# First stage of a graph kernel: message products in quarters of the PE array, with a new order of PE's work

## The reference

```
h = silu(edge_attr_16 @ Wfc1/4);   w = h @ Wfc2/8          # 192 weights: w0, w1 (64 each), w2, w3 (32 each)
e0 = (x0 @ Wl1_0 * a / 8)[src];    e1 = (x1 @ Wl1_1 * a / sqrt(32))[src]
mid0 = w0 * e0 * sh0;              mid1 = w3 * (e1 . sh1) / sqrt(3)
mid2 = w1 * e0 * sh1;              mid3 = w2 * e1 * sh0
```

## Time and profile before

| | us |
|---|---|
| median of 3 runs | 903.74 (903.16 to 905.57) |
| profiled execution: time | 900.12 |
| its span | 898.4 |
| PE busy | 845.2 (94%) |
| DVE busy | 810.1 (90%) |
| POOL busy | 713.5 (79%) |
| ACT busy | 628.3 (70%) |

### The profile page before, as it was taken

How to read it: one execution, slowest core, us unless ns; L and a number is a source line. 1 busy time by engine, 2 the same in 40 slices (tenths; PEclk the granted TensorE clock), 3 DMA queues, 4 the chain that set the end, 5 groups by cost and what they waited for, 6 DMA issues and landing times.

```text
span 898.4 us, 33828 instructions
## 1 busy us (share of the span) xinstructions
PE 845.2 (94%) x11276; PEld 713.2 (79%) x11276; DVE 810.1 (90%) x2797; ACT 628.3 (70%) x1961; POOL 713.5 (79%) x804
## 2 busy tenths in 40 slices
PE   2999899999999999999999988999999999999994
PEld 1788788888887887888888877888888888888884
DVE  3798899999998999999999987999999999999997
ACT  1555455555555555565565554999999999999998
POOL 6777777777777776777777711999999999999995
PEclk9999999999999999999999999999999999999998
DMA  6455544544557676557764412899999999999994
GB/s 184 122 169 168 153 134 137 139 129 130 133 145 151 187 209 182 174 163 204 210 179 133 130 69 101 249 307 311 317 299 309 332 332 305 311 319 307 316 310 159
DMA packets 87544, 186.85 MB, mean 208 GB/s; under 512 B 17646, under 2 KB 48138, under 8 KB 87371
## 3 DMA queue, kind: packets, MB, share of 16 engines
q1 hardware_dynamic: 50715, 93.00, 31.9%
q0 software_dynamic: 18944, 35.81, 18.1%
q10 hardware_dynamic: 17712, 55.87, 18.1%
HBM read 119.66 MB, written 64.95 MB: 205 GB/s over the span
## 4 chain that ended last, share of the span: by engine, by line
PE 50%; DVE 14%; SPq 12%; issue 12%; DMA 6%; POOL 4%; ACT 2%; DVEq 0%; ACTq 0%; POOLq 0%
PE ps L831 9%; SPq L467 9%; PE ps L772 7%; PE ps L751 6%; PE ps L732 5%; PE ps L769 5%; PE ps L738 5%; DVE mid L1024 4%; PE ps L817 3%; SPq L457 3%; DVE z L1042 3%; PE ps L714 3%; PE ps L847 3%; PE ps L712 3%; POOL gat L620 2%
## 5 line engine op out<-in xcount | busy, mean ns | idle before, releaser
L620 POOL DMA_INDIRECT gat<-turned,srcs x196 | 192.2, 981 | 65.6 <-issue 61.2
L620 POOL DMA_INDIRECT gat<-spread,srcs x196 | 187.7, 958 | 62.4 <-issue 59.1
L901 ACT ACTIVATE te<-ps 128x512 f32<-128x512 f32 x196 | 106.4, 595 | 123.7 <-PE ps L738 120.8
L831 PE MATMUL ps<-win,eas 60*128 60x162 f32 x2352 | 190.0, 306 | 1.1 <-DVE eas L1367 0.7
L772 PE MATMUL ps<-wy,mid 128*128 128x161 f32 x784 | 182.3, 314 | 0.0
L831 PEld LDWEIGHTS ps<-win,eas 60*128 60x128 f32 x2352 | 165.6, 186 | 18.0 <-DVE eas L1367 11.0
L1048 DVE SCALAR_TENSOR_TENSOR msg<-ps,sha,z 128x161 f32<-128x161 f32 x392 | 151.0, 385 | 13.9
L686 POOL TENSOR_TENSOR gat<-eas,gat 128x640 f32<-128x640 f32 x98 | 152.0, 1551 | 10.9 <-ACT eas L946 10.5
L769 PE MATMUL ps<-wy,mid 128*128 128x97 f32 x784 | 141.6, 262 | 0.2 <-DVE mid L1024 0.2
L1024 DVE TENSOR_TENSOR mid<-ps,te 128x512 f32<-128x512 f32 x196 | 133.3, 680 | 3.3 <-PE ps L751 3.3
L924 ACT ACTIVATE te<-gat,shift,rstd 128x160 f32<-128x160 f32 x292 | 131.8, 533 | 2.7 <-DVE shift L1314 1.3
(11 more groups left out here) (110 smaller groups left out, 1501.1 us busy)
## 6 DMA issues: line engine op xcount, KB each, us to landing
win<-rows SPq DMA_DIRECT2D x392, 114.6 KB, 4.0
rows<-msg SPq DMA_DIRECT2D x98, 326.0 KB
out<-te ACTq DMA_DIRECT2D x47, 640.0 KB, 6.6
xin<-x_g ACTq DMA_DIRECT2D x76, 322.0 KB, 5.7
kept_x<-x_g SPq DMA_DIRECT2D x16, 322.0 KB
gat<-turned,srcs POOLq DMA_INDIRECT x196
gat<-spread,srcs POOLq DMA_INDIRECT x196
eas<-ea_t SPq DMA_DIRECT2D x7, 384.0 KB, 3.8
```

What stands on the lines that cost most here:

```text
L620: pool.indirect_dma_start(out=gat[:, slot, first:first + of.shape[1]], out_offset=None, in_=of, in_offset=bass.IndirectOffsetOnAxis(ap=src ...
L831: last = nc.tensor.matmul(agg_ps[b1][:, 2 * h + k, 0:SW], hot[side(h), b1, k, c, :], win[side(h), (RING * i + b - 1) % WIN_RING, k, c, 0:S ...
L901: nc.scalar.activation(e_sb[:, t, :], e_ps[:, t], ACT.Copy).then_inc(e_out[t], 1)
```

## The change

**PE, y products.** `combine` cuts each product of a tile into quarters: rows of the weights' input in two halves, and edges in two halves. Products with zero blocks of the weights are left out. A pair takes 16 products of 64 rows by 64 edges with 32, 66 or 99 columns. The outputs lie in banks 6 and 7, in 16 lanes of 33 numbers (`CHUNK`), the two tiles' lanes in turn; a product writes one, two or three lanes. Products from the lower half of the rows write bank 6, those from the upper half bank 7.

**Banks and waits.** Both pairs use banks 6 and 7, so `combine` waits for the messages of the pair just before it (`msg_ready[t], p`). The banks of e hold nothing else, and e waits for no message.

**Order on PE.** y of pair 0, first layer, transposes of both pairs, y of pair 1, e, w. On ACT `take_second` stands ahead of `take_turned`; on DVE both `multiply` follow `finish` of pair 0.

**ACT and DVE.** `take_second` copies 132 numbers for both tiles at once. `finish` makes two products for a pair, 128 and 64 numbers (32 for each tile and component), and then one message product for each tile. A message is 165 numbers wide, five chunks of 32 and one (count, label, gate, one unused), where it was 163; the label is written into `z` and goes through the message product. The node stage multiplies 164 columns in L831, and ACT takes the 160 sums out of five chunks. Tables, weights and the output's columns are put in another order outside the kernel's loops.

```
-GATE, CNT, LABEL = 0, 1 + D, 2 + D
-SW = 2 + D
-AW = 3 + D
+CHUNK = MUL1 + 1
+CHUNKS = 5
+AW = CHUNKS * CHUNK
+SW = AW - 1
+
+
+M_A, M_C, M_S, M_B = 0, CHUNK, 2 * CHUNK, 4 * CHUNK
+CNT, LABEL, GATE = M_A + MUL1, M_C + MUL1, M_S + MUL1
...
-        y_ps = [ps[:, n:n + 2, 0:YW] for n in (2, 6)]
-        heads_ps = ps[:, 6:8, YW:YW + T // 2]
-        wrong_ps = ps[0:1, 6, YW + T // 2:YW + T // 2 + 1]
+        heads_ps = ps[:, 6:8, 0:T // 2]
+        wrong_ps = ps[0:1, 6, T // 2:T // 2 + 1]
+
+        y_ps = ps[:, 6:8, :].rearrange("p c e -> p (c e)")
+
+        def y_at(t, j, count=1, every=1):
+
+            flat = y_ps
+            lanes = flat[:, 512 - YB:512 + YB].rearrange("p (j t w) -> p j t w", t=2, w=CHUNK)
+            return lanes[:, j + 4:j + 4 + (count - 1) * every + 1:every, t, :]
...
+            def find_e(q):
+                b = q % 2
+
+                pe.wait_ge(t_out, 2 * q + 2)
+                if q >= 1:
+                    for t in range(2):
+                        pe.wait_ge(e_out[t], q)
+                for n in range(2):
+                    for t in range(2):
...
             def combine(q, k):
-                p, y = 2 * q + k, y_ps[k]
-                if p == 1:
+                p = 2 * q + k
+                if p == 0:
                     pe.wait_ge(heads_out, 2)
+                    pe.wait_ge(wy_ready, 12)
                 for t in range(2):
-                    if p == 0:
-                        pe.wait_ge(wy_ready, 12)
                     pe.wait_ge(mid_ready[t], q + 1)
-                    if k == 0:
-                        pe.wait_ge(e_out[t], min(q + 2, NS))
-                    if q >= 1:
-                        pe.wait_ge(msg_ready[t], p - 1)
-                    nc.tensor.matmul(y[:, t, 0:W_Y1 - W_YA], mid[:, q % 2, t, 0, k, :],
-                                     wy[:, 0:W_Y1 - W_YA], start=True, stop=True)
-                    of = (W_Y1, W_Y1B)[t] - W_YA
-                    nc.tensor.matmul(y[:, t, W_Y1 - W_YA:YW], mid[:, q % 2, t, 1, k, :],
-                                     wy[:, of:of + VEC + 1 + MUL0],
-                                     start=True, stop=True).then_inc(y_ready[t], 1)
+                    if p >= 1:
+                        pe.wait_ge(msg_ready[t], p)
+
+
+                low, high = slice(0, HALF), slice(HALF, P)
+                made = ((0, 0, low, W_V, y_at(0, -4)[:, :, 0:MUL1]),
+                        (0, 0, high, W_YA, y_at(0, 1, 2)),
+                        (0, 1, low, W_Y1, y_at(0, -3, 3)),
+                        (0, 1, high, W_Y1, y_at(0, 0, 2, 3)),
+                        (1, 0, low, W_YA, y_at(1, -2, 2)),
+                        (1, 0, high, W_V, y_at(1, 3)[:, :, 0:MUL1]),
+                        (1, 1, low, W_Y1B, y_at(1, -4, 2)),
+                        (1, 1, high, W_Y1B, y_at(1, 0, 3)))
+                for t, c, half, w, y in made:
+                    width = y.shape[1] * y.shape[2]
+                    for edges in (low, high):
+                        last = nc.tensor.matmul(
+                            y[edges], mid[half, q % 2, t, c, k, edges],
+                            wy[half, w - W_YA:w - W_YA + width].rearrange(
+                                "p (j w) -> p j w", j=y.shape[1]), start=True, stop=True)
+                last.then_inc(y_ready, 1)
 
             def step(d):
+                if alive(d, 3):
+                    combine(d - 3, 0)
                 if alive(d, 0):
                     first_layer(d)
-                for k in range(2):
-                    if alive(d, 0):
+                    for k in range(2):
                         turn(d, k)
-                    if alive(d, 3):
-                        combine(d - 3, k)
+                if alive(d, 3):
+                    combine(d - 3, 1)
                 if alive(d, 1):
-                    weigh(d - 1)
+                    find_e(d - 1)
+                    find_w(d - 1)
...
             def take_second(q, k):
                 p = 2 * q + k
-                for t in range(2):
-                    act.wait_ge(y_ready[t], p + 1)
-                    if p >= 2:
+                act.wait_ge(y_ready, p + 1)
+                if p >= 2:
+                    for t in range(2):
                         act.wait_ge(msg_ready[t], p - 1)
-                    nc.scalar.activation(z[:, k, t, 0:1 + MUL0], y_ps[k][:, t, Y_C:YW],
-                                         ACT.Copy).then_inc(zc_ready[t], 1)
+                flat = y_ps
+                first, other = 512 - 3 * LANES, 512 + LANES + CHUNK
+                c = flat[:, first:first + 2 * (other - first)].rearrange(
+                    "p (t w) -> p t w", t=2)[:, :, 0:2 * LANES].rearrange(
+                    "p t (j w) -> p t j w", j=2)[:, :, :, 0:CHUNK]
+                nc.scalar.activation(
+                    z[:, k, :, M_S:M_B].rearrange("p t (j w) -> p t j w", j=2), c,
+                    ACT.Copy).then_inc(zc_ready, 1)
 
             def step(d):
                 for k in range(2):
+                    if alive(d, 3):
+                        take_second(d - 3, k)
                     if alive(d, 0):
                         take_turned(d, k)
-                    if alive(d, 3):
-                        take_second(d - 3, k)
...
             def label(q):
-                half = slice(q % 2 * QUAD, (q % 2 + 1) * QUAD)
-                if q >= 2:
+                if q >= 1:
+                    for t in range(2):
+                        dve.wait_ge(msg_ready[t], 2 * q)
+                nc.vector.tensor_copy(
+                    z[:, :, :, LABEL],
+                    dsts[:, QUAD * q:QUAD * (q + 1)].rearrange("p (k t) -> p k t", t=2)
+                ).then_inc(label_ready, 1)
+
+            def finish(q, k):
+                p, ring = 2 * q + k, q % SHA_RING
+                pair = slice(2 * k, 2 * k + 2)
+                flat = y_ps
+                first, other = 512 - 4 * LANES, 512 + 3 * LANES + CHUNK
+                v = flat[:, first:first + other - first + MUL1]
+                dve.wait_ge(zc_ready, p + 1)
+                if p >= 2:
+                    for t in range(2):
+                        dve.wait_ge(msg_ready[t], p - 1)
+                spread = sha[:, ring, pair, :].rearrange("p t m -> p (t m)")
+                nc.vector.tensor_tensor(
+                    z[:, k, :, M_A:M_S].rearrange("p t (j w) -> p t j w", j=2)[:, :, :, 0:MUL1],
+                    two_of(v, other - first, MUL1).unsqueeze(2).broadcast_to([P, 2, 2, MUL1]),
+                    two_of(spread[:, 1:], 5, 2).unsqueeze(3).broadcast_to([P, 2, 2, MUL1]),
+                    ALU.mult).then_inc(zb_ready, 1)
+                nc.vector.tensor_tensor(
+                    z[:, k, :, M_B:M_B + MUL1],
+                    two_of(v, other - first, MUL1),
+                    two_of(spread[:, 3:], 2, 1).broadcast_to([P, 2, MUL1]),
+                    ALU.mult).then_inc(zb_ready, 1)
+                if k == 0 and q >= 2:
                     dve.wait_ge(messages_out[q % 2], 16 * (q // 2))
-                nc.vector.tensor_copy(msg[:, half, LABEL], dsts[:, QUAD * q:QUAD * (q + 1)]
-                                      ).then_inc(label_ready, 1)
-
-            def finish(q, k):
-                p, ring, y = 2 * q + k, q % SHA_RING, y_ps[k]
+                dve.wait_ge(label_ready, q + 1)
+                dve.wait_ge(zb_ready, 2 * p + 2)
                 for t in range(2):
                     n = 2 * k + t
-                    dve.wait_ge(zc_ready[t], p + 1)
-                    if p >= 2:
-                        dve.wait_ge(msg_ready[t], p - 1)
-                    nc.vector.tensor_tensor(
-                        z[:, k, t, 1 + MUL0:].rearrange("p (m v) -> p m v", m=3),
-                        y[:, t, 0:MUL1].unsqueeze(1).broadcast_to([P, 3, MUL1]),
-                        sha[:, ring, n, 1:4].unsqueeze(2).broadcast_to([P, 3, MUL1]),
-                        ALU.mult).then_inc(zb_ready[t], 1)
-                    dve.wait_ge(zb_ready[t], p + 1)
+                    y = y_at(t, (-1, -4)[t], CHUNKS)
                     nc.vector.scalar_tensor_tensor(
-                        out=msg[:, q % 2 * QUAD + n, 0:1 + D], in0=y[:, t, Y_A:Y_C],
-                        scalar=sha[:, ring, n, 0:1], in1=z[:, k, t, :],
+                        out=msg[:, q % 2 * QUAD + n, :].rearrange("p (j w) -> p j w", w=CHUNK),
+                        in0=y, scalar=sha[:, ring, n, 0:1],
+                        in1=z[:, k, t, :].rearrange("p (j w) -> p j w", w=CHUNK),
                         op0=ALU.mult, op1=ALU.add).then_inc(msg_ready[t], 1)
 
             def step(d):
-                if alive(d, 2):
-                    multiply(d - 2, 0)
                 if alive(d, 3):
                     label(d - 3)
                     finish(d - 3, 0)
                 if alive(d, 2):
-                    multiply(d - 2, 1)
+                    for t in range(2):
+                        multiply(d - 2, t)
                 if alive(d, 3):
```

146 lines of the change are left out of this document (80 added, 66 removed).

## The result

| | before | after |
|---|---|---|
| median of 20 runs each, us | 905.66 (898.06 to 913.42) | 916.12 (907.90 to 922.73) |
| ratio of the times | | 1.0103, 95% interval 1.0072 to 1.0134 |
| profiled execution (its span) | 900.12 (898.4) | 918.41 (916.7) |
| PE, DVE, POOL, ACT busy | 94, 90, 79, 70% | 87, 87, 78, 66% |

The changed kernel is slower by 1.0%, some 10 us. The profiled pair lies 18.3 us apart, since the profile of before is 5.5 us under its median and that of after 2.3 above. So the traces tell where the time lies, and the medians how much it is.

What follows compares the result with a forecast made beforehand. PE was taken to bound the edge stage, with DVE and POOL's gathers close behind. Steps falling from 5.22 to 5.01 us (-17.4), tail +2.7 + 1.5 and node stage +2.2 gave -11.0: 892.7 us, likeliest case 888 to 900, range 883 to 919.

Steps and rivals of the forecast that it cites:

- The hand-over's terms: Edge stage, y burst's start to next burst's earliest start through PE, ACT and DVE: 2.31 us, within a cycle of 5.01.
- cost and gain nothing on this path: Edge-stage step: moving the label into z and dropping e's wait for the messages were said to change nothing.
- the balance rival: Edge steps of 5.10 to 5.17 us cancel against 6.4 us of cost outside them: 902 to 907 us, chance 0.13.
- What extra work DVE has in some 35 steps costs as now: Edge stage: DVE's additional work in some 35 steps was said to cost the same after the change as before.
- What bounds the kernel before: Edge stage: the chain of one step was read as PE alone, 5.23 us between e products, commonest 5.22.
- 4.7 us for PE's own work after the change: Edge-stage step: PE's own work, with shorter y products and more changes of shape, was put at about 4.7 us.
- Burst, PE's wait, PE's work: Edge step: burst 0.58 us to next line, 0.75 to end; PE waits 0.5 before second burst, then works 2.70.
- products that write with gaps: Rival on y quarters: gapped writes don't overlap, a burst takes 1.05 us instead of 0.58, kernel 985 us; chance 0.05.
- The tail: End of edge stage, after the last e products: 11.3 us instead of 8.6, +2.7, with +1.5 more in the sum.
- the +1.5 that the sum has for the clock: Term added to the tail's +2.7 in the sum; a granted clock below 1 was expected only near the edge stage's end.
- The node stage: L831 multiplies 164 columns instead of 162: 0.023 us a group in 98 groups, +2.2 us, range 0 to 4.
- hand-over longer than PE's work: Rival for the edge steps: hand-over becomes the bound, longer bursts and DVE products, 5.3 us a step, 917 us; chance 0.23.

Runs made afterwards that it cites:

- experiment 1: Each kernel with one more DVE product a step (before 926.3 us, changed 951.6), or with three PE transposes of pair 1 made twice (before 913.5, changed 914.7).
- experiment 6: Changed kernel with eleven unread transposes in each of PE's last waits: 916.5 us; kernel before with 165-column message rows: 904.2 us in one execution.

## Why the prediction was wrong

The forecast was 892.7 us and faster by 1.2%; it is slower by 1.0%. By the medians that is +10.5 us for -11.0, 21.5 apart. Against the profiled execution of before the sum was -11.0 and the trace says +18.3, 29.3 apart (31.5 but for the earlier first step), some of it chance of that pair.

Two steps of the prediction failed, and they are 16 of the 21.5 us:

- **The hand-over's terms: right chain, wrong size, 2.53 us and not 2.31.** 0.12 between `z` and the messages, where I took 0.03 for an instruction that must wait, and left out the wait for the label that its move into `z` puts there ("cost and gain nothing on this path"); 0.14 from DVE's end to PE, where I took 0.06 from one row; 0.05 in small pieces. With the 0.10 less of the other half that is 5.13 instead of 5.01, **10 us** on 83 steps. By the prediction's own sum 5.13 gives 902.6: no change worth the name, as in the balance rival.
- **"What extra work DVE has in some 35 steps costs as now": it costs more, 6 us.** I gave DVE 4.8 us a step and two loops of it a reserve of 0.2. It has 4.98 and waits inside the loop. Before, 0.23 of each one-off piece were covered (experiment 1); after, nearly nothing. In the 26 steps with such work the excess over the commonest is 10.8 us, where it was 4.8. This, with what the write at 276 us costs, turns no change into a loss.

The other parts:

- **What bounds the kernel before: not PE alone.** The prediction read the chain of a step as PE's alone. PE's own work was 5.10 us, and 0.12 a wait of e for the messages (experiment 1). Its 4.7 us for PE's own work after the change came near (5.13 - 0.54 = 4.59), but the ordinary step was bound by a hand-over before and after.
- **Burst, PE's wait, PE's work: right.** The burst took 0.54 to the next line (0.58 said, from an assumption on how the quarters take turns that no trace here shows) and 0.75 to the end, the wait was 0.54 (0.5 said), and products that write with gaps went as fast as those without: 0.54 us for 263 columns a quarter, where L847 took 0.52 for 256. e, w and burst took 2.60 (2.70 said).
- **Steps over the commonest: +17.3 us in the profiled pair.** 7.7 belong to the stall at 276 us, 3.2 to PE's stall at 314 us with the half clock behind it, 6.0 to DVE's one-off work, 0.8 to the first step (gathers) and some 3 to small excesses in other steps; against them stand the 3.4 by which before lost more at 514 us. The stall at 276 us was not foreseen. The forecast is added to the median of before, which has in it what the write costs there, so only what it costs more in the changed kernel is missing, some 6 us in the profiles and unexplained.
- **The tail: right.** +4.3 against +4.2, hand-overs of 2.5 and two bursts at half clock, though PE waited there three times and not four. No run shows the +1.5 that the sum has for the clock; in its place the half clock was worth 2.9 us in the traces (experiment 6), 1.0 of it in the two bursts (1.26 and 1.27 us for 0.75).
- **The node stage: not told apart.** +6.4 against +2.2 in the profiled pair, but some 1 us in the means of nineteen traces.

The rival "hand-over longer than PE's work" gave 917 by steps of 5.3 us; the mean step is 5.45, the commonest 5.13. So its time came by luck and its mechanism is half right: no burst took longer after a wait (0.75 us with the 0.54 ahead of it and without), the DVE products with gaps 0.01 and not 0.05 more, but hand-overs and DVE decide, as it said.
